# Last stage of a two-layer kernel: early loads, pair exchange moved into the key-value sums, variance floor added on GpSimd

## The reference, cut to what matters

```
q = gelu(xn @ Wq.T + bq) + 0.21          # k likewise
q_r, k_r = rope(q), rope(k)              # out[2i] = a*cos - b*sin, out[2i+1] = b*cos + a*sin
z = 1 / (q . mean(k) + 1e-6)             # per head and token
kv = sum_n k_r[n] v[n] / 2048            # per head, 16 x 16
s = layernorm((q_r @ kv) * z + xn, eps 1e-12) * gamma + beta
g = silu(moe(xn))                        # 64 experts, 6 a token, plus a shared one
x = x + s * g
```

## Time and profile before

| | |
|---|---|
| time, median of 3 runs | 5831.89 us (5829.03 to 5831.96) |
| profiled execution, its own time | 5830.87 us |
| its span, first to last instruction | 5829.2 us |
| busy, whole span | PE 88%, PEld 52%, DVE 74%, ACT 51%, POOL 51% |
| mean granted clock of TensorE | 0.94 of 2.4 GHz |
| last stage | begins at 5545.79 us, 283 us long |

### The profile page before, as it was taken

How to read it: one execution, slowest core, us unless ns; L and a number is a source line. 1 busy time by engine, 2 the same in 40 slices (tenths; PEclk the granted TensorE clock), 3 DMA queues, 4 the chain that set the end, 5 groups by cost and what they waited for, 6 DMA issues and landing times. The chain is left out here.

```text
span 5829.2 us, 79896 instructions
## 1 busy us (share of the span) xinstructions
PE 5125.5 (88%) x26190; PEld 3043.6 (52%) x26190; DVE 4295.0 (74%) x8755; ACT 2984.0 (51%) x6297; POOL 2987.4 (51%) x1603
## 2 busy tenths in 40 slices
PE   7778778777785799998999899999989998998877
PEld 2222223222221577776555566666655555666745
DVE  3999999999999688887333477777753338994258
ACT  4776776776775577775111355555531114442233
POOL 4999899889989455554111344444421110004724
PEclk9888998999986899999999999999999999999988
DMA  5556556566654222222111111111111116444565
GB/s 134 143 149 149 140 146 149 129 144 155 146 132 101 82 86 87 88 88 78 48 54 51 49 34 34 34 35 36 34 53 55 54 40 208 150 145 134 143 208 181
DMA packets 503856, 598.14 MB, mean 103 GB/s; under 512 B 59782, under 2 KB 381332, under 8 KB 499348
## 3 DMA queue, kind: packets, MB, share of 16 engines
q1 hardware_dynamic: 484308, 582.36, 36.4%
q10 hardware_dynamic: 6848, 8.67, 0.5%
q0 software_dynamic: 12288, 2.00, 0.3%
HBM read 429.38 MB, written 180.37 MB: 105 GB/s over the span
## 5 line engine op out<-in xcount | busy, mean ns | idle before, releaser
L654 POOL TENSOR_TENSOR db<-durep,brep 128x2048 f32<-128x2048 f32 x256 | 1161.5, 4537 | 188.6 <-DVE p_h L561 178.1
L513 ACT ACTIVATE p_h<-dlrep,am 128x512 f32<-128x512 f32 x1024 | 704.5, 691 | 196.3 <-DVE hh L572 171.2
L561 DVE TENSOR_TENSOR_SCAN p_h<-p_h,hlast,db 128x512 f32<-128x512 f32 x576 | 720.6, 1284 | 0.0
L1213 POOL TENSOR_TENSOR rn<-n,mhalf 128x16 f32<-128x16 f32 x128 | 375.1, 2931 | 629.0 <-DVE n L1160 628.9
L349 PE MATMUL p_acc<-hh,fold 128*32 128x512 f32 x2048 | 317.2, 696 | 342.9 <-DVE hh L572 341.5
L572 DVE TENSOR_TENSOR hh<-p_h,crep 128x512 f32<-128x512 f32 x768 | 520.9, 678 | 0.0
L1538 POOL TENSOR_TENSOR grstd<-grstd,mhalf 128x4 f32<-128x4 f32 x32 | 32.6, 1020 | 789.3 <-DVE grstd L1465 789.3
L1217 POOL TENSOR_TENSOR rot_cos<-rot_cos,rot_sin 128x1024 f32<-128x1024 f32 x128 | 302.2, 2361 | 220.3 <-DVE rot_sin L1150 220.3
L946 PE MATMUL p_o<-probT,v 128*64 128x128 f32 x4096 | 406.0, 279 | 7.6 <-DVE probT L1133 3.8
L1030 ACT ACTIVATE probT<-p_t 128x512 f32<-128x512 f32 x256 | 152.9, 597 | 481.5 <-PE p_t L933 481.5
L946 PEld LDWEIGHTS p_o<-probT,v 128*64 128x64 f32 x4096 | 344.2, 137 | 91.7 <-issue 70.7
(11 more groups left out here) (278 smaller groups left out, 11923.2 us busy)
## 6 DMA issues: line engine op xcount, KB each, us to landing
dlrep<-delta_rows SPq DMA_DIRECT2D x256, 256.0 KB
durep<-drive_rows SPq DMA_DIRECT2D x256, 256.0 KB
ew<-in_L_ffn_w SPq DMA_DIRECT2D x192, 176.0 KB
first_queries_keys<-qs SPq DMA_DIRECT2D x128, 256.0 KB, 2.1
qk<-first_queries_keys SPq DMA_DIRECT2D x64, 512.0 KB, 3.8
brep<-bc_rows SPq DMA_DIRECT2D x64, 256.0 KB
crep<-bc_rows SPq DMA_DIRECT2D x64, 256.0 KB
delta_rows<-dl SPq DMA_DIRECT2D x64, 256.0 KB
```

The source lines that it names most:

```text
L513: act.activation(p_h[:, (i % BANKS) * CH:(i % BANKS + 1) * CH], dlrep[use % 2][:, j], ACT.Exp, scale=am[:, q, j, g:g + 1]).then_inc(s_ex, 1)
L561: dve.tensor_tensor_scan(out=state, data0=bank, data1=db[s % 2][:, j], initial=0.0 if first else hlast[:, i % TILES:i % TILES + 1], op0=AL ...
L654: pool.tensor_tensor(out=db[s % 2][:], in0=durep[use % 2][:], in1=brep[c % 2][:, g:g + 1, :].to_broadcast([P, 4, CH]), op=ALU.mult).then_i ...
L1213: pool.tensor_tensor(out=rn[f % 2][:], in0=n2[f % 2][:], in1=mhalf[:], op=ALU.pow).then_inc(s_rn, 1)
```

## The change

- A class `FirstTiles` allocates buffers and semaphores that live through `experts` and `final`, in a context around both. SyncE issues, inside its loop over the experts, `last_stage_weights()` after the weights of expert 16 (query weights, bias row, blocks, gamma, beta) and `last_stage_chunk(f)` after those of experts 24 and 32 (rope rows, turned rows, key-value sums, `xn` and `x1` of chunks 0 and 1). `ym` and `yo` of these chunks are loaded in `final`, as they are complete only then.
- In `final` SyncE's order is now: ym and yo of chunk 0, cs 2 (which waits for the transposes of table 0), ym and yo of chunk 1, rows 2, rows 3; cs 3 after the store of chunk 0, as before.
- The exchange of pairs moves to the key-value sums. `swap` is minus the identity with neighbouring columns exchanged; `key_means(b)` on TensorE has one more product, `swap` with the sums, and VectorE copies it to `kvx`. `attend` multiplies the cosine half with `kv` and the sine half with `kvx`. The second weights, biases, queries and Gelus go: `queries` fills two banks, 2c and 2c+1 modulo 4, and both rotations read the same `qT`.
- The add of 1e-12 moves from VectorE's `moments` to the head of GpSimd's `power`.

```diff
-        with nc.cleanup_on_exit(), ExitStack() as ctx:
-            experts(...)
-        with nc.cleanup_on_exit(), ExitStack() as ctx:
-            final(...)
+        with nc.cleanup_on_exit(), ExitStack() as both:
+            first = FirstTiles(nc, both)
+            with nc.cleanup_on_exit(), ExitStack() as ctx:
+                experts(..., first)
+            with nc.cleanup_on_exit(), ExitStack() as ctx:
+                final(..., first)
...
+            def last_stage_chunk(f):
+                rowsf = slice(f * CH, (f + 1) * CH)
+                sp.dma_start(first.cs[f][:], A["c_rope"][rowsf, :].rearrange(
+                    "(j p) (a d) -> p j a d", p=P, a=2)).then_inc(first.s_cs[f], 16)
+                sp.dma_start(first.xT[f][:].rearrange("p f t -> p (f t)"),
+                             xt_d[f * P:(f + 1) * P, :]).then_inc(first.s_xT[f], 16)
+                sp.dma_start(first.kv[f][:], kv_d[f * P:(f + 1) * P, :]).then_inc(first.s_kv[f], 16)
+                sp.dma_start(first.xn[f][:], tiles(xe_d[rowsf, 0:D])).then_inc(first.s_xn[f], 16)
+                sp.dma_start(first.x1[f][:], tiles(x1_d[rowsf, :])).then_inc(first.s_x1[f], 16)
...
+                if e == 2 * U:
+                    last_stage_weights()
+                if e in (3 * U, 4 * U):
+                    last_stage_chunk(e // U - 3)
...
+            load_sums(0)
+            load_cs(2)
+            load_sums(1)
             load_rows(2)
             for c in range(NC):
-                if c + 2 < CPB:
-                    load_cs(c + 2)
+                if c == 1:
+                    load_cs(3)
...
             def queries(c):
                 pe.wait_ge(s_xT[c % 2], 16 * (c // 2 + 1))
-                for q in range(4):
-                    pe.wait_ge(s_empty, fills(c) - 4 + q + 1)
-                    f = q % 2
+                for f in range(DH):
+                    if c < CPB or c == CPB:
+                        pe.wait_ge(s_empty, tables_at(min(c, CPB - 1)) + bank(c, f) + 1)
+                    else:
+                        pe.wait_ge(s_empty, queries_at(c - 2) + f + 1)
                     for h in range(DH):
-                        ins = pe.matmul(p_q[q][:], w_q[q // 2][:, h, f * P:(f + 1) * P], xT[c % 2][:, h, :],
+                        ins = pe.matmul(p_q[bank(c, f)][:], w_q[:, h, f * P:(f + 1) * P], xT[c % 2][:, h, :],
...
-                ins.then_inc(s_kmt, 1)
+                    pe.transpose(p_x[:, f * P:(f + 1) * P], kv[b % 2][:, D + f * P:D + (f + 1) * P], ident[:])
+                pe.matmul(p_x[:, D:2 * D], swap[:], kv[b % 2][:, 0:D], start=True, stop=True).then_inc(s_kmt, 1)
...
                         for a in range(2):
                             ins = pe.matmul(p_o[:, at:at + P], rot[k][a][:, f, j * P:(j + 1) * P],
-                                            kv[b % 2][:, f * P:(f + 1) * P], start=(a == 0), stop=(a == 1))
+                                            (kv, kvx)[a][b % 2][:, f * P:(f + 1) * P], start=(a == 0), stop=(a == 1))
...
-                ins.then_inc(s_km, 1)
+                if b > 1:
+                    dve.wait_ge(s_o, CPB * (b - 1))
+                dve.tensor_copy(kvx[k][:], p_x[:, D:2 * D]).then_inc(s_km, 1)
...
-                dve.wait_ge(s_mv, c + 1)
-                dve.tensor_scalar(rs[k][:], mv[k][:, :, 1:2], 1e-12, None, ALU.add).then_inc(s_va, 1)
...
             def power(c):
+                if c > 1:
+                    pool.wait_ge(s_be, c - 1)
+                pool.wait_ge(s_mv, c + 1)
+                pool.tensor_scalar(rs[c % 2][:], mv[c % 2][:, :, 1:2], 1e-12, None, ALU.add).then_inc(s_va, 1)
                 pool.wait_ge(s_va, c + 1)
                 pool.tensor_tensor(out=rs[c % 2][:].rearrange("p j a -> p (j a)"),
```

More of the change, by code:

```diff
@@ L2115, with __init__, experts @@
 RLOADS = 12
-def experts(nc, ctx, A, xe_d, y_d, odd_d, take, put, ident):
+class FirstTiles:
+    def __init__(self, nc, ctx):
+        sb, ps, sem = allocators(nc, ctx)
+        self.cs = [sb(f"fcs{k}", [P, CT, 2, D]) for k in range(2)]
+        self.xT = [sb(f"fxT{k}", [P, DH, CH]) for k in range(2)]
+        self.kv = [sb(f"fkv{k}", [P, 2 * D]) for k in range(2)]
+        self.xn, self.x1 = ([sb(f"{n}{k}", [P, CT, D]) for k in range(2)] for n in ("fxn", "fx1"))
+        self.w_q, self.brow, self.blk = sb("w_q", [P, DH, D]), sb("fbrow", [P, D]), sb("fblk", [P, P])
+        self.gam, self.bet = sb("gam", [P, D]), sb("bet", [P, D])
+        self.s_w, self.s_blk, self.s_gb = sem("f_weights"), sem("f_blk"), sem("f_gamma_beta")
+        self.s_cs, self.s_xT, self.s_kv, self.s_xn, self.s_x1 = (
+            [sem(f"f_{n}{k}") for k in range(2)] for n in ("cs", "xT", "kv", "xn", "x1"))
+def experts(nc, ctx, A, x1_d, xe_d, xt_d, y_d, odd_d, kv_d, take, put, ident, first):
     sb, ps, sem = allocators(nc, ctx)
@@ L2261, in final @@
     p_o, p_z, p_x = ps("fp_o", CT * D), ps("fp_z", 512), ps("fp_x", 512)
-    s_w, s_blk, s_kv = sem("f_weights"), sem("f_blk"), [sem(f"f_kv{k}") for k in range(2)]
-    s_xn, s_x1, s_ym, s_yo = ([sem(f"f_{n}{k}") for k in range(NB)] for n in ("xn", "x1", "ym", "yo"))
-    s_xT, s_cs, s_out = ([sem(f"f_{n}{k}") for k in range(2)] for n in ("xT", "cs", "out"))
+    s_w, s_blk, s_gb, s_kv, s_xT, s_cs = first.s_w, first.s_blk, first.s_gb, first.s_kv, first.s_xT, first.s_cs
+    s_xn, s_x1 = (t + [sem(f"f_{n}{k}") for k in range(2, NB)] for t, n in ((first.s_xn, "xn"), (first.s_x1, "x1")))
+    s_ym, s_yo = ([sem(f"f_{n}{k}") for k in range(NB)] for n in ("ym", "yo"))
+    s_out = [sem(f"f_out{k}") for k in range(2)]
     s_swap, s_bias, s_bq, s_kmt, s_km, s_ksum, s_cst = (
@@ L2378, in _ @@
             pe.wait_ge(s_w, 32)
-            pe.wait_ge(s_swap, 2)
-            for k in range(2):
-                for f in range(DH):
-                    ins = pe.transpose(p_x[:, (2 * k + f) * P:(2 * k + f + 1) * P], brow[k][:, f * P:(f + 1) * P], ident[:])
+            for f in range(DH):
+                ins = pe.transpose(p_x[:, f * P:(f + 1) * P], brow[:, f * P:(f + 1) * P], ident[:])
             ins.then_inc(s_bias, 1)
@@ L2411, in queries @@
                     act.wait_ge(s_rot, c - 1)
-                for q in range(4):
-                    act.wait_ge(s_fill, fills(c) + q + 1)
-                    act.activation(qT[k][q // 2][:, q % 2, :], p_q[q][:], ACT.Gelu,
-                                   bias=b_q[:, q:q + 1]).then_inc(s_empty, 1)
+                for f in range(DH):
+                    act.wait_ge(s_fill, queries_at(c) + f + 1)
+                    act.activation(qT[k][:, f, :], p_q[bank(c, f)][:], ACT.Gelu, bias=b_q[:, f:f + 1]).then_inc(s_empty, 1)
                 if c + 2 < NC:
@@ L2513, in finish @@
                     dve.wait_ge(s_out[k], 16 * (c // 2))
+                if c == 0:
+                    dve.wait_ge(s_gb, 32)
                 dve.wait_ge(s_mv, c + 1)
```

93 lines of the change are left out of this document (44 added, 49 removed).

## The result

The kernel after runs in 5817.41 us (median of 14 runs, 5813.23 to 5819.72), against 5830.34 us for the kernel before on the same chip (14 runs, 5825.77 to 5833.11): ratio 0.9978, 95% interval 0.9970 to 0.9986. That is 12.9 us faster; 5820.5 was forecast. Its profiled execution took 5817.33 us, span 5815.6.

The account below looks back on a forecast made before the run. VectorE sets mid-stage pace, after waits for transfers at the last stage's opening; -22.5 + 0.5 + 0 + 10.5 - 0.3 + 0.7 = -11.1 against 5830.87 gives 5819.8, forecast as 5820.5 us, range 5804 to 5828.

Parts of the forecast that it names:

- the likeliest case: The forecast mechanism, VectorE and GpSimd waiting for each other in mid-stage: chance 0.60, own range 5815 to 5826 us.
- The front: Opening of the last stage: earlier transfers and 8 query records for 16 start rotate(3) at 5606.5 instead of 5628.99, -22.5 us.
- Exchange in the sums: Last stage: fewer query products gain 0 in mid-stage; the swap product costs +0.5 us in chunk 2, 0 at later switches.
- the half-clock stretch is already paid: At the two later key-value switches TensorE already runs at half clock, so the exchange adds 0 there (bounds -1 and +4).
- 1e-12 to GpSimd: Mid-stage: the moved add makes join end later and hold fo + fxn 1.05 us in ten chunks, +10.5 us.
- Last chunk: In the last chunk no rotation follows: the moved add saves 0.6, the final scale waits about 0.3, so -0.3 us.
- Clean-up: At the kernel's end: one more clean-up, +0.7 us.
- The transfers beside the experts: Expert stage: the last stage's early loads fit beside the experts and cost 0; uncovered at most 16 us.
- the third rival: Expert stage: early transfers not free, GpSimd's scatters delayed, experts end up to 8 us later: 5828 us, chance 0.08.
- the cover: Expert stage: weights issued eight experts ahead (29 us) and gathers six (22 us) hide the early transfers.
- no mutual waiting: Mid-stage: the rotation starts under GpSimd's residual, each chunk loses 0.68 us, period 12.09: 5806 us, chance 0.22.
- Half clock: Mid-stage: TensorE, with less work, stays at 1.2 GHz, making a chunk 17.6 us: 5857 us, chance 0.10.

Follow-up runs that it names:

- e10: The kernel before with the early transfers alone, without the exchange in the sums and with the add of 1e-12 on VectorE: 5817.5 us, ratio 0.9984.
- e1: The kernel after with the add of 1e-12 moved back to VectorE, all else as changed: 5811.1 us, ratio 0.9976.
- e9: The kernel after with GpSimd's addition of the residual over two of four tiles, leaving out the other half: 5805.2 us, ratio 0.9966.
- e5: The kernel after with GpSimd's join over two of its four tiles, leaving out half of the sum: 5807.7 us, ratio 0.9970.
- e4: The kernel before with only the add of 1e-12 moved to GpSimd: 5833.3 us, ratio 1.0012.
- e12: The kernel after with last table and later key-value sums asked for early and the add of 1e-12 on VectorE; transfers in two bursts: 5786.2 us, ratio 0.9930.
- e6: The kernel after with its ten chunk transfers issued one at every fourth expert instead of in two bursts of five: 5812.8 us, ratio 0.9976.

## Why the prediction was right, and where its sizes were off

The forecast was 5820.5 and the time is 5817.4, inside the likeliest case's own range. The mechanism that it called decisive held: in after, ten chunks, and just the ten it named, have `fo + fxn` at 2.08 to 2.11 us. Term by term:

- **The front, -22.5.** Measured from the last `eyb` to `rotate(3)`, -24.3, inside the bounds of -19 and -26. The steps came in the forecast order and close to the forecast times: the first table at 5548.06 behind the opening, the last table issued at 5590.77, `rotate(3)` at 5606.79. That the last two agree within 0.3 us is partly luck: the stage opened at 5548.0 and not at the assumed 5545.8, and counted from there `rotate(3)` came 58.8 us later where 60.7 was worked out. e10 shows that it is two gains: 12.2 us by the early transfers alone (92.6 to 80.4), 12.2 by the exchange and what comes with it (80.4 to 68.3). The prediction had the second inside the first, by counting 8 records for 16.
- **Exchange in the sums, +0.5 and then 0 at the switches.** +0.2 in chunk 2. At the two later switches the sum with the add's part was 0.0 and +3.4 us in after. For the exchange alone it is +7.0 (e10 to e1), outside the bounds of -1 and +4. The step that failed is "the half-clock stretch is already paid": TensorE, which had 2.99 us of idle time there in the kernel before, has 10.81 in after, and its work behind the landing takes 2.2 us longer in e1 than in e10; 1.3 us more are the transfer's own. The prediction did say that shorter work would not bring the transfer sooner; it gave that too little weight.
- **1e-12 to GpSimd, +10.5.** The cost of a chunk was 0.80 us, not 1.05: the held `fo + fxn` ends 1.08 us after `join` (5773.73 - 5772.65), where one issued freely takes 1.23, and the pow needs less time behind the second rotation. The count was ten and had to be seven, for the output of a chunk ahead of a switch waits for TensorE anyway and chunk 14 is followed by no full one. Seven times 0.80 is +5.6. Between the bounds of -6.8 and +23 the middle way, the whole wait, was right: e9 shows it for the rotation, e5 for `fo + fxn`.
- **Last chunk, -0.3.** From fo15 to the end, moving the add saves 0.7 us (e4 against before) and 0.5 (after against e1), a little more than forecast.
- **Clean-up, +0.7.** The kernels with the additional block and the add on VectorE, e1 and e10, take 0.2 and 0.3 us more than before from fo15 to the end, and SyncE has one more wait of 0.4 us at a clean-up there. So it costs less than half of the forecast. Together with the last chunk the measured difference is -0.3, against a forecast of +0.4. At the opening nothing is added: from the last `eyb` to SyncE's first transfer of the stage it is 9.51 us in after and 9.39 before.
- **The transfers beside the experts, 0.** This is the step that failed. It was +6.5 us in the profile, the third rival's mechanism, which had a chance of 0.08 and a price of up to 8. The step was the cover: "gathers six (22 us)". The gather of expert 29 is issued only 9.9 us ahead of its pair in the kernel before and 5.4 us ahead in after, because GpSimd issues it behind its scatters, and with two bursts of five transfers 27 us apart those land late. So the rival was right in naming the scatters; TensorE then waited for the gathers behind them.
- **In sum:** -24.3 + 0.2 + 8.7 - 0.3 + 6.5 = -9.2 for the stretches that the change touches, -13.6 in the two spans with the 4.4 us by which the work ahead of it happened to be shorter. Errors of opposite sign cancelled in part: 6.5 for the experts and 3.4 at the switches were taken as nothing, about 5 too much stood for the add and 2 too little for the front. That the number came close is partly luck. (The recorded sum gives 5819.8 + 1.0 = 5820.8, not the 5820.5 that was forecast, which changes nothing here.) The sign that was given for the third rival, an experts' end later than 5541, failed to show it: the last `eyb` starts at 5538.5, since the work ahead of the experts happened to be 4.4 us shorter. The length of the stage shows it.

Of the rivals, *no mutual waiting* is wrong by e9: issued with the residual just over, the same two rotations take 2.33 us, where with it running they take 3.07. *Half clock* is right as an observation and wrong as a bound: TensorE's clock is 0.90 on the mean in mid-stage and its z products take 3.19 us for 16 after 4.40 of idle time, yet VectorE's waits for it are four in the whole stage, 11.8 us, against five and 10.0 before. The row of one of those chunks:

```profile
5756.13 3.19 PE L2409 MATMUL fp_z<-fkm,fqT 128*128 128x8 f32 x16 [4.40 <-DVE zz L2519]
```

The Trainium skill, "SBUF — State Buffer", "Who interferes with whom", says that a VectorE instruction with two SBUF inputs excludes a GpSimd instruction that reads SBUF and that the order of issue decides who waits. e5 and e9 agree where GpSimd issues first: once GpSimd's instruction is over, the held one is back at 1.23 us, and at 2.33 beside 2.35. For the other direction the trace of after agrees: GpSimd's add takes 1.20 us when issued inside a rotation and 0.23 without one. The same section of the Trainium skill also lists the tensor_scalar among the operations that can take the shared ports when its operands allow it; the 0.75 and 1.39 us of `frs` and `fcst` in e12 agree.

What stays open: whether spreading the transfers shortens the run as it shortens the experts. The profiles say 3.3 to 6 us, the ratios 1 to 7, less than their uncertainty. Whether a single burst, or a smaller one, would cost anything was not tried either. Open too is why the key-value sum's transfer takes 8.4 to 9.0 us in after and e1 and 7.2 to 7.3 in e10; no run tried it.

## What to carry to other kernels

When a chunk is bound by two engines that exclude each other, an instruction moved from one to the other is not worth its own duration: it moves the point at which the next exclusion begins. Lay the two timelines side by side and follow who is issued first. When work is taken off an engine that waits for a transfer, its wait grows unless the transfer's issue moves too (here from 2.45 to 8.95 us), and nothing is gained: 23 us lay in issuing one table and two sums earlier, more than in the whole change. Transfers put beside a stage with room on the DMA engines belong there one at a time: the same ten cost 3 to 6 us in two bursts and at most 2 spread out. And the lead of a transfer is read from the trace, from its issue to its use, and not from the loop distance in the program: six experts were 22 us on paper and 10 in the trace.

## What the runs showed of the hardware that was not expected

- A one-input VectorE tensor_scalar on 4 columns, which takes 0.17 us alone, waits for GpSimd's instruction on 1024 columns as a two-input one does: 0.75 us for `frs`, 1.39 for `fcst` on 16 columns. GpSimd's own add on 4 columns takes 0.23 us alone and 1.20 behind a rotation.
- With the DMA engines full for 45 us (share 0.96 to 1.06), GpSimd waited up to 3.04 us at a time for its scatters to land, gathers came up to 1.27 us too late, and TensorE, after three such waits, fell to 1.2 GHz for a time (mean granted clock 0.72 over 12 us). Twelve us of full DMA engines did not do it: in e6 the share is 0.96 from 5430 to 5442 and no gather is late.
- After 2.45 us of idle time the sixteen z products took 3.42 us, as after 8.95 us; in the first chunk of after, at a granted clock of 1.00, 1.85 us.
